# The seam between two layers of a graph network: part of the next matrix ahead of the last row tile, other work moved between the outputs

## The chip, the cores and the metric

The kernel runs on one core of one Trainium2 chip. The metric is the device time in microseconds (us) of one execution; the time of a kernel is the median of several runs.

## The reference, cut to what matters

625 nodes with 768 features pass four residual layers. Layers 0, 1 and 3 are graph attention layers, layer 2 is three relational convolutions. Every layer begins with a normalization of the whole input row, so a row tile of the next layer's input exists only when that row tile of this layer's output does.

```python
h = jnp.maximum(_layernorm(x, axis=-1), 0.0)
x = x + _L1_gnn_ref(h, edge_index, ...)            # attention, 4 heads of 512, then 1 head of 768
h = jnp.maximum(_layernorm(x, axis=-1), 0.0)
x = x + _L2_gnn_ref(h, node_type_3, edge_index, edge_type_3, ...)
# in _L2: h = concat([x, node_emb[node_type]], -1); then three times
xw = jnp.einsum('nd,rde->rne', h, w_rel)           # 3 relations
msg = xw[edge_type, src] * inv[dst, edge_type][:, None]
h = relu(segment_sum(msg, dst) + h @ w_root + bias)
```

## The kernel before

The 625 nodes are five row tiles of 125. Edges have been counted into dense matrices, so aggregation is a matrix product. Float32 products are split in a high and a low part: ACT copies the high part (lines L1131 for weights, L1247 for layer inputs), POOL subtracts the low part of weights (L1042), DVE the low part of everything that comes out of PSUM (L1451), and TensorE (PE) multiplies three times.

One list of steps (`STEPS`) is walked by all engines, each taking its own part of every step **in the order of the list**. No scheduler moves anything: an engine that waits for one step does nothing of a later one. `gat_steps` writes the list of an attention layer, and its last phase is the seam of this case. For the last head each row tile `t` goes through `mask_rows`, `score_rows` (DVE, L1795 and L1803), `softmax` (ACT exp, L1287) and `attention_T` (PE transposes, L786; ACT and DVE copy into `AT`). `tick` writes these for one `t`, `attention_T` coming three ticks behind. Then for each tile `d` come two steps:

- `output` d: PE multiplies (L832, 30 matmuls). ACT has a DMA bring the old x of tile d+1 into one of two buffers `xl`; POOL adds the bias (L1095); DVE makes the new rows `xo` (L1848) and their statistics; POOL makes the scale (`nb`, L1074); ACT makes the normalized rows `hn` (L1174) and stores x.
- `norm_T` d: PE transposes `hn` (L842, and in layer 1 also L847, which picks two nodes), ACT copies the high part and DVE the low part into `XB` (layer 0) or `XA` (layer 1). The low part of a tile raises "input lo" for it.

In the list `output` d+1 stands ahead of `norm_T` d. So on ACT the rows `hn` of tile 4 stand ahead of the high part of tile 3. The matrix of the next layer (L756) begins when all five tiles are there: 240 matmuls of 256 columns after layer 0, and after layer 1 the step `relation` 0 of the first convolution, 105 matmuls of 384 columns. Between layer 1 and `relation` 0 stands `embed`: DVE makes the operands of the node type embedding in a dozen small instructions (from L1860), PE multiplies them (L900), ACT and DVE put the result into `XA`, and then DVE counts the columns of relation 0 (`count_columns`, L1516 and L1502), ahead of the low part of the rows of `relation` 0 (`Hl`, L1451). PE needs the PSUM banks that this last step frees for the transposes `degrees` (L793) and the counted columns for `mean_T`, which come next.

Weights come through a ring `stage` (three tiles of 384) and a ring `pairs` (five tiles of 384); the step `split` says how far ACT and POOL may split them. In layer 1 all five are split at tick 5. At `output` 0 of layer 1 ACT also starts the DMA `cr_in` (2.3 MB of edge counts) in the same queue as the x tiles.

## Time and profile before

| | us |
|---|---|
| median of 3 runs | 1867.71 |
| range of the runs | 1866.33 to 1869.11 |
| the profiled execution: its own time | 1865.71 |
| its span | 1863.9 |
| PE busy | 1560.5 |
| DVE busy | 859.0 |
| ACT busy | 585.0 |
| POOL busy | 533.1 |

The span is what the profile's rows lie in. 1.8 us of the own time lie around it. Starts in the rows are us from the start of the span.

### The profile page before, as it was taken

What the parts mean: (1) busy time and instruction counts of PE and PEld (TensorE: products, weight loads), DVE (VectorE), ACT (ScalarE), POOL (GpSimd) and SP (SyncE); (2) the same over time, 40 slices, a digit from 0 to 9 for tenths busy, and PEclk for the clock granted to TensorE, in tenths of its full rate; (3) what the DMA queues carried; (4) which work ended last, traced back from release to release, by engine and by line L of the source; (5) the groups of instructions that cost most, each with busy time, mean ns of one, the idle gap of its engine ahead of it and who ended that gap; (6) DMA issues with size and microseconds to landing.
All of it is one profiled execution on the core that took longest, in us unless ns stands there. A gap on an engine that the chain in (4) does not pass through costs nothing.

```text
span 1863.9 us, 27128 instructions
## 1 busy us (share of the span) xinstructions
PE 1560.5 (84%) x10165; PEld 1505.3 (81%) x10165; DVE 859.0 (46%) x2156; ACT 585.0 (31%) x1170; POOL 533.1 (29%) x681
## 2 busy tenths in 40 slices
PE   4985889996778898975999999999999996566777
PEld 3655889996778898975999999999999986456777
DVE  5786676314266763144644223140423133677633
ACT  2224343322234433222332222322221222355421
POOL 3233332232233322313222333323231322222122
PEclk9997899997888999986999999999999997767797
DMA  2221111122211101222111122112123222100012
GB/s 87 72 75 37 44 46 29 45 76 62 75 51 46 46 29 46 75 80 87 48 30 49 52 60 61 55 52 58 57 61 86 74 88 72 31 1 1 5 47 86
DMA packets 87923, 101.63 MB, mean 55 GB/s; under 512 B 9477, under 2 KB 80418, under 8 KB 87796
## 3 DMA queue, kind: packets, MB, share of 16 engines
q1 hardware_dynamic: 71290, 68.86, 12.8%
q10 hardware_dynamic: 16506, 31.07, 5.0%
q8 instruction: 81, 1.33, 0.3%
q14 instruction: 46, 0.38, 0.1%
HBM read 88.12 MB, written 11.78 MB: 54 GB/s over the span
## 4 chain that ended last, share of the span: by engine, by line
PE 62%; DVE 11%; issue 9%; DMA 7%; ACT 6%; POOL 3%; ACTq 0%; DVEq 0%; POOLq 0%; SPq 0%
PE ps L756 35%; PE ps L819 7%; PE ps L931 6%; PE ps L913 4%; DMA xl<-x_scratch 3%; PE ps L786 3%; DVE junk L1748 2%; DVE prob L1795 2%; PE ps L889 2%; DMA stage<-in_W 2%; DMA xl<-in_x 1%; PE ps L952 1%; POOL pairs L1042 1%; ACT pairs L1131 1%; PE ps L975 1%
## 5 line engine op out<-in xcount | busy, mean ns | idle before, releaser
L1042 POOL TENSOR_TENSOR pairs<-stage,pairs 128x256 fp32r<-128x256 f32 (+3 forms) x472 | 367.0, 795 | 891.5 <-ACT pairs L1131 890.5
L756 PE MATMUL ps<-pairs,XB 128*125 128x256 f32 (+2 forms) x2880 | 424.2, 309 | 23.2 <-issue 8.1
L756 PEld LDWEIGHTS ps<-pairs,XB 128*125 128x125 f32 (+1 forms) x2880 | 413.9, 197 | 27.5 <-issue 10.2
L756 PE MATMUL ps<-pairs,XA 128*125 128x256 f32 (+3 forms) x2655 | 378.0, 304 | 7.1 <-DVE asp L1748 6.0
L756 PEld LDWEIGHTS ps<-pairs,XA 128*125 128x125 f32 (+2 forms) x2655 | 373.1, 190 | 9.2 <-DVE asp L1748 6.4
L1131 ACT ACTIVATE pairs<-stage 128x256 fp32r<-128x256 f32 (+3 forms) x472 | 189.7, 424 | 580.8 <-PE ps L756 416.5
L819 PE MATMUL ps<-AT,Hg 125*128 125x314 f32 (+1 forms) x1080 | 168.3, 317 | 13.9 <-ACT asb L1272 7.3
L819 PEld LDWEIGHTS ps<-AT,Hg 125*128 125x128 f32 (+1 forms) x1080 | 162.7, 191 | 15.8 <-ACT asb L1272 8.1
L1451 DVE TENSOR_TENSOR Hl<-ps,Hl 125x768 fp32r<-125x768 f32 (+3 forms) x57 | 43.6, 818 | 271.0 <-ACT Hl L1181 271.0
L786 PE MATMUL ps<-ident,prob 125*125 125x125 f32 x475 | 89.8, 348 | 85.9 <-ACT full L1189 33.2
L786 PEld LDWEIGHTS ps<-ident,prob 125*125 125x125 f32 x475 | 80.5, 253 | 92.0 <-issue 39.8
L1089 POOL TENSOR_SCALAR prob<-prob,rden 125x625 f32<-125x625 f32 x80 | 81.0, 1012 | 227.2 <-DVE rden L1811 227.2
L931 PE MATMUL ps<-MT,Hl 125*128 125x314 f32 (+1 forms) x780 | 115.4, 308 | 0.0
L931 PEld LDWEIGHTS ps<-MT,Hl 125*128 125x128 f32 (+1 forms) x780 | 113.8, 189 | 0.0
L832 PE MATMUL ps<-Hg,AT 125*125 125x384 f32 x450 | 90.7, 363 | 9.4 <-DVE AT L1451 9.4
L832 PEld LDWEIGHTS ps<-Hg,AT 125*125 125x125 f32 x450 | 86.6, 204 | 10.7 <-issue 8.3
L1451 DVE TENSOR_TENSOR Hg<-ps,Hg 125x1024 fp32r<-125x1024 f32 (+3 forms) x24 | 18.6, 819 | 157.9 <-ACT Hg L1181 157.9
L1795 DVE SCALAR_TENSOR_TENSOR prob<-asb,ad 125x626 f32<-125x626 f32 x95 | 85.0, 895 | 12.7 <-ACT asb L1272 12.7
L1803 DVE CUSTOM_DVE_ANT_0 prob<-prob,lnc 125x626 f32<-125x626 f32 x95 | 87.2, 918 | 1.6
L1451 DVE TENSOR_TENSOR AT<-ps,AT 125x625 fp32r<-125x625 f32 x75 | 58.4, 800 | 62.4 <-ACT AT L1215 62.4
L1287 ACT ACTIVATE prob<-prob,mx 125x626 f32<-125x626 f32 x95 | 77.1, 812 | 31.7 <-DVE mx L1803 21.3
L1897 DVE TENSOR_TENSOR scaled<-ps,degrees 128x628 f32<-128x628 f32 x39 | 31.6, 810 | 105.0 <-PE ps L931 104.9
(210 smaller groups left out, 1696.5 us busy)
## 6 DMA issues: line engine op xcount, KB each, us to landing
stage<-in_W SPq DMA_DIRECT2D x192, 128.0 KB, 2.3
stage<-in_rel SPq DMA_DIRECT2D x99, 192.0 KB, 2.4
stage<-in_root SPq DMA_DIRECT2D x91, 64.0 KB, 1.8
x_scratch<-xo ACTq DMA_DIRECT2D x15, 375.0 KB
xl<-x_scratch ACTq DMA_DIRECT2D x15, 375.0 KB
stage<-in_rel SPq DMA_DIRECT2D x42, 128.0 KB, 2.1
stage<-in_root SPq DMA_DIRECT2D x12, 192.0 KB, 2.4
stage<-in_W SPq DMA_DIRECT2D x12, 192.0 KB, 2.5
```

Of the source, the lines that this page charges most:

```text
L756: last = mm(o, X[:rows, xi, a, P * (s0 + t):P * (s0 + t) + m], pair(n, b), start=k == 0 and i == 0 and t * pitch % BANK == 0, stop=k == le ...
L786: last = nc.tensor.transpose(slot(q)[:m, 128 * j:128 * j + P], M[:, d, P * j:P * j + m], ident[:P, :P])
L819: last = mm(halves(q, m)[:, c, :], Hg[:, t, a, c0:c0 + m], att_of(l, h)[:P, t, b, HC * c:HC * c + HC], start=t == 0 and i == 0, stop=t == ...
L832: last = mm(halves(q, P, 384)[:, c, :], AT[:, t, a, P * d:P * d + P], Hg[:, t, b, 384 * c:384 * c + 384], start=t == 0 and i == 0, stop=t ...
L931: last = mm(halves(q, 128)[:, half, :], Hl[:rows, t, r, a, 128 * f:128 * f + 128], MT[:rows, r, t, HC * half:HC * half + HC], start=t == 0 ...
L1042: nc.gpsimd.tensor_tensor(pair(n, 1), staged(n), pair(n, 0).bitcast(F32), ALU.subtract).then_inc(*up("weights_lo", "weights lo", n))
L1089: nc.gpsimd.tensor_scalar(prob[:, d, :N], prob[:, d, :N], rden[:, d:d + 1], 1.0, ALU.mult, ALU.mult).then_inc(*up("prob_ready", "rows read ...
L1131: A(pair(n, 0), staged(n), ACT.Copy).then_inc(*up("weights_hi", "weights hi", n))
L1287: A(prob[:, d, :N + 1], prob[:, d, :N + 1], ACT.Exp, bias=mx[:, d:d + 1], scale=-1.0, accum_out=den[:, d:d + 1]).then_inc(*up("exp_ready", ...
L1451: return V.tensor_tensor(out_ap, whole, hi_ap.bitcast(F32), ALU.subtract)
L1795: V.scalar_tensor_tensor(out=prob[:, d, :N + 1], in0=asb[:, 0, :N + 1], scalar=ad8[:, heads_order[l, h] % 2, d:d + 1], in1=asb[:, 1, :N + ...
L1803: V.tensor_tensor_reduce(out=prob[:, d, :N + 1], in0=prob[:, d, :N + 1], in1=lnc[:, d, :N + 1], scale=-1.0, scalar=-FLOOR, op0=ALU.add, op ...
```

## The change

The list of steps is written differently at the ends of layers 0 and 1; nothing is computed differently.

- `early`: the first matrix of the next layer begins with its first four weight tiles (`EARLY_K`) on row tiles 0 to 3, after `norm_T` 3 and ahead of `norm_T` 4. `late` does these four weight tiles for row tile 4 after `norm_T` 4; the rest follows as before. `early` does not signal its weights as used, `late` does.
- The lag of `attention_T` is two ticks and not three, in layers 0 and 1.
- In layer 1 three tiles of relation weights are split after tick 1 (`split_to`), the other two at tick 5 as before.
- In layer 1 the operands of the embedding are made between `output` 3 and `output` 4 (`embed_operands`) with their own buffers. The product, its copy and `count_columns` stay in `embed`.

```diff
@@ gat_steps @@
-    for t in range(NT + 3):
-        yield from tick(l, h, t)
+    lag = 3 if l == 3 else 2
+    for t in range(NT + lag):
+        yield from tick(l, h, t, lag)
+        if l == 1 and t == 1:
+            yield ("split_to", ("relation", 1, 0, 0, 384), STAGED // WMAX)
         if l == 1 and t == 5:
             yield ("split", ("relation", 1, 0, 0, 384), 0)
         if t >= 4:
             yield ("output", l, t - 4)
             if t > 4 and l != 3:
                 yield ("norm_T", l + 1, t - 5)
-    yield ("output", l, NT - 1)
+    for d in range(NT + lag - 4, NT):
+        if l == 1 and d == NT - 1:
+            yield ("embed_operands",)
+        yield ("output", l, d)
+        if l != 3 and d < NT - 1:
+            yield ("norm_T", l + 1, d - 1)
     if l != 3:
+        first = FIRST_MATRIX[l + 1]
         yield ("norm_T", l + 1, NT - 2)
+        yield ("early", first)
         yield ("norm_T", l + 1, NT - 1)
+        yield ("late", first)
@@ PE @@
+                                if g == mine[0]:
+                                    ready = source_ready(s, k)
+                                    if kind == "early":
+                                        ready = (*ready[:2], NT - 2)
...
-                        else:
+                        elif kind != "early":
                             last.then_inc(*up("weights_used", "weights used", n))
@@ DVE @@
-                elif kind == "embed":
+                elif kind == "embed_operands":
                     dve.wait_ge(*at("node ids"))
...
                     V.tensor_copy(nth[:, N:N + CLONES], most[:R, :]).then_inc(*up("embed", "embed operands"))
+                elif kind == "embed":
+                    V.memset(degrees[:, :, N:NP], 0.0)
                     V.memset(XA[:, 0:6, :, N + CLONES:NP].bitcast(F32), 0.0).then_inc(*up("embed", "XA pad"))
                     dve.wait_ge(*at("embed hi"))
```

**What stands where, PE.** The end of layer 1 on PE before, from `output` 4 to the end of `relation` 0; a row is line, operation, written tile and read tiles, shape and count. `hn` is transposed in `norm_T` 3 and then 4, L900 is the embedding's product.

```order
L832 MATMUL ps<-Hg,AT 125x384 x30
L842 MATMUL ps<-ident,hn 128x125 x6
L847 MATMUL ps<-pickc,hn 128x2 x6
L842 MATMUL ps<-ident,hn 128x125 x6
L847 MATMUL ps<-pickc,hn 128x2 x6
L900 MATMUL ps<-nth,emh 128x314 x4
L756 MATMUL ps<-pairs,XA 125x384 x24
```

The same place now.

```order
L867 MATMUL ps<-Hg,AT 125x384 x30
L877 MATMUL ps<-ident,hn 128x125 x6
L882 MATMUL ps<-pickc,hn 128x2 x6
L791 MATMUL ps<-pairs,XA 125x384 x48
L877 MATMUL ps<-ident,hn 128x125 x6
L882 MATMUL ps<-pickc,hn 128x2 x6
L791 MATMUL ps<-pairs,XA 127x384 x12
L935 MATMUL ps<-nth,emh 128x314 x4
```

48 matmuls stand ahead of `norm_T` 4, and the embedding's product comes behind the 12 of row tile 4. After layer 0 it is the same with 48 and 12 matmuls of 256 columns, without L882 and L935.

**What stands where, DVE.** The end of layer 1 on DVE before, from `xo` of tile 4: statistics, low part of tile 3, low part of tile 4, and the first rows of the embedding's operands.

```order
L1848 SCALAR_TENSOR_TENSOR xo<-ps,rden,xl 125x768
L1436 BN_STATS bns<-xo 125x6 x2
L1439 BN_AGGR mv<-bns 125x2
L1571 TENSOR_TENSOR xc<-ps,xc 128x12
L1451 TENSOR_TENSOR XA<-ps,XA 128x6x125
L1571 TENSOR_TENSOR xc<-ps,xc 128x12
L1451 TENSOR_TENSOR XA<-ps,XA 128x6x125
L1583 CAST XA<-xc 128x6x2
L1451 TENSOR_TENSOR XA<-xc,XA 128x6x2
L1860 CAST scaled<-node_74 128x628
```

The last row of the operands now (the others stand ahead of it), and what follows.

```order
L1913 CAST nth<-most 3x2
L1883 SCALAR_TENSOR_TENSOR xo<-ps,rden,xl 125x768
L1471 BN_STATS bns<-xo 125x6 x2
L1474 BN_AGGR mv<-bns 125x2
L1606 TENSOR_TENSOR xc<-ps,xc 128x12
L1486 TENSOR_TENSOR XA<-ps,XA 128x6x125
L1606 TENSOR_TENSOR xc<-ps,xc 128x12
L1486 TENSOR_TENSOR XA<-ps,XA 128x6x125
L1618 CAST XA<-xc 128x6x2
L1486 TENSOR_TENSOR XA<-xc,XA 128x6x2
L1915 MEMSET degrees 128x3x3
L1916 MEMSET XA 128x12
```

The operands moved ahead of `xo` of tile 4. The embedding's copy and the counting of columns still come behind all of this.

**What stands where, ACT.** The last rows of layer 1 on ACT now: high part of tile 2, `hn` of tile 4, its store, and the high parts of tiles 3 and 4. Before it was the same order.

```order
L1282 ACTIVATE XA<-ps 128x6x125
L1209 ACTIVATE hn<-xo,nb,rstd 125x768
L1201 DMA x_scratch<-xo 125x768
L1282 ACTIVATE XA<-ps 128x6x125 x2
L1404 ACTIVATE XA<-ps 128x628
```

Nothing moved here: the high part of tile 3, for which `early` waits, stands behind `hn` of tile 4.

## Rows read from the trace of the kernel before

**Rows 1.** the page: first line, and the chain that ended last, by line

```profile
span 1863.9 us, 27128 instructions
...
PE ps L756 35%; PE ps L819 7%; PE ps L931 6%; PE ps L913 4%; DMA xl<-x_scratch 3%; PE ps L786 3%; DVE junk L1748 2%; DVE prob L1795 2%; PE ps L889 2%; DMA stage<-in_W 2%; DMA xl<-in_x 1%; PE ps L952 1%; POOL pairs L1042 1%; ACT pairs L1131 1%; PE ps L975 1%
```

**Rows 2.** PE in time, end of layer 0: start, length, what, [idle before]

```profile
447.93 8.10 PE L832 MATMUL ps<-Hg,AT 125*125 125x384 f32 x30 [2.51 <-DVE AT L1451]
...
492.55 1.49 PE L842 MATMUL ps<-ident,hn 125*128 125x125 f32 x6 [7.45 <-ACT hn L1174]
495.95 31.09 PE L756 MATMUL ps<-pairs,XB 128*125 128x256 f32 x240 [1.92 <-DVE XB L1451]
```

**Rows 3.** ACT in order of time, end of layer 0

```profile
491.38 1.03 ACT L1174 ACTIVATE hn<-xo,nb,rstd 125x768 f32<-125x768 f32 x1 [7.10 <-POOL nb L1074]
...
492.31 0.78 ACT L1247 ACTIVATE XB<-ps 128x750 fp32r<-128x750 f32 x1
```

**Rows 4.** DVE in order of time, end of layer 0

```profile
493.12 0.94 DVE L1451 TENSOR_TENSOR XB<-ps,XB 128x750 fp32r<-128x750 f32 x1 [3.17 <-ACT XB L1247]
```

**Rows 5.** chain that ended last, in order of time, layer 0

```profile
475.77 9.90 DMA xl<-in_x
```

**Rows 6.** busy time, PEclk and DMA in stretches of 10 us

```profile
500.00:510.00 10.00, 10.00 (x81) 10.00 (x81) 0.00 (x0) 2.54 (x7) 3.36 (x5) 0.93 0.19 54
910.00:920.00 10.00, 9.83 (x59) 9.60 (x60) 8.07 (x21) 5.54 (x14) 0.00 (x0) 0.83 0.07 22
```

**Rows 7.** PE in order of time, end of layer 1 and relation 0

```profile
855.20 1.39 PE L786 MATMUL ps<-ident,prob 125*125 125x125 f32 x5
856.25 7.12 PE L832 MATMUL ps<-Hg,AT 125*125 125x384 f32 x30
...
871.09 1.40 PE L847 MATMUL ps<-pickc,hn 125*128 125x2 f32 x12
...
886.33 1.38 PE L900 MATMUL ps<-nth,emh 3*128 3x314 f32 x4 [6.88 <-DVE XA L1880]
887.64 20.05 PE L756 MATMUL ps<-pairs,XA 128*125 128x384 f32 x105
...
910.05 2.12 PE L793 MATMUL ps<-ident,inv 125*128 125x125 f32 x10 [1.83 <-DVE Hl L1451]
...
915.81 18.73 PE L756 MATMUL ps<-pairs,XA 128*125 128x384 f32 x105
```

**Rows 8.** DVE in order of time, end of layer 1 and relation 0

```profile
869.04 0.93 DVE L1451 TENSOR_TENSOR XA<-ps,XA 128x750 fp32r<-128x750 f32 x1
870.70 1.02 DVE L1848 SCALAR_TENSOR_TENSOR xo<-ps,rden,xl 125x768 f32<-125x768 f32 x1 [0.73 <-issue]
...
876.27 0.93 DVE L1451 TENSOR_TENSOR XA<-ps,XA 128x750 fp32r<-128x750 f32 x1
...
881.54 0.48 DVE L1860 CAST scaled<-node 128x628 f32<-128x628 int32 x1
...
888.47 0.81 DVE L1451 TENSOR_TENSOR XA<-ps,XA 128x628 fp32r<-128x628 f32 x1 [2.27 <-ACT XA L1369]
...
902.10 0.23 DVE L1525 SCALAR_TENSOR_TENSOR mean<-mean,once,column 125x5 f32<-125x5 f32 x1
909.04 2.29 DVE L1451 TENSOR_TENSOR Hl<-ps,Hl 125x768 fp32r<-125x768 f32 x3 [6.71 <-ACT Hl L1181]
```

**Rows 9.** DVE in order of time, start of layer 1's last phase

```profile
819.05 2.00 DVE L1803 CUSTOM_DVE_ANT_0 prob<-prob,lnc 125x626 f32<-125x626 f32 x1
```

**Rows 10.** POOL in order of time, the same place

```profile
818.57 1.81 POOL L1095 TENSOR_TENSOR xl<-xl,b2b 125x768 f32<-125x768 f32 x1 [25.97 <-DMA xl<-x_scratch]
```

**Rows 11.** chain that ended last, in order of time, layer 1

```profile
818.07 26.54 DMA xl<-x_scratch
```

**Rows 12.** ACT in order of time, end of layer 1

```profile
874.44 1.03 ACT L1174 ACTIVATE hn<-xo,nb,rstd 125x768 f32<-125x768 f32 x1 [5.52 <-POOL nb L1074]
...
875.37 0.78 ACT L1247 ACTIVATE XA<-ps 128x750 fp32r<-128x750 f32 x1
```

More of the change, by code:

```diff
@@ L42 @@
 PASSES = ((0, 0), (0, 1), (1, 0))
+EARLY_K = 4
+FIRST_MATRIX = {1: ("project", 1, 0, 256), 2: ("relation", 1, 0, 0, 384)}
 EXACT = 4096.0
@@ L84, in tick @@
         yield ("softmax", l, h, t - 1)
-    if 3 <= t < NT + 3:
-        yield ("attention_T", l, h, t - 3)
+    if lag <= t < NT + lag:
+        yield ("attention_T", l, h, t - lag)
 def rows_of(s):
@@ L324, in weight_tiles, with begin @@
 def weight_tiles(I):
-    out, begun = {}, {}
+    out, begun = {}, dict.fromkeys(FIRST_MATRIX.values(), EARLY_K)
+    def begin(s, tiles):
+        if s in FIRST_MATRIX.values():
+            out["early", s] = tiles[:EARLY_K]
     for l, (heads, dh) in GAT_HEADS.items():
@@ L339, in weight_tiles @@
             if s[0] in ("project", "project2"):
+                begin(s, tiles)
                 k0, k1 = part or (begun.get(s, 0), len(tiles))
@@ L346, in weight_tiles @@
             f0 = RGCN_CHUNKS[i][c][0]
-            out[s] = [(I[f"rel_{i}"][r, 128 * k:128 * k + 128, f0:f0 + w], 128, w) for k in range(RGCN_IN[i])]
+            tiles = [(I[f"rel_{i}"][r, 128 * k:128 * k + 128, f0:f0 + w], 128, w) for k in range(RGCN_IN[i])]
+            begin(s, tiles)
+            out[s] = tiles[begun.get(s, 0):]
         if s[0] == "combine":
@@ L364, in build @@
         for s in STEPS:
-            whole = s[1] if s[0] == "part" else s
+            whole = s[1] if s[0] in ("part", "early") else s
             first_tile.setdefault(whole, len(W))
@@ L370, in build @@
                 begun[whole] = s[3]
+            if s[0] == "early":
+                begun[whole] = EARLY_K
         def ring(columns):
@@ L398, in split_limit @@
         def split_limit(s):
+            if s[0] == "split_to":
+                return first_tile[s[1]] + s[2]
             if s[0] == "split":
@@ L724, in _ @@
                 kind = s[0]
-                if kind in ("project", "project2", "relation", "part"):
-                    k_from, k_to = s[2:] if kind == "part" else (begun.get(s, 0), None)
-                    if kind == "part":
+                if kind in ("project", "project2", "relation", "part", "early", "late"):
+                    k_from, k_to = ((0, EARLY_K) if kind in ("early", "late") else
+                                    s[2:] if kind == "part" else (begun.get(s, 0), None))
+                    if kind in ("part", "early", "late"):
                         s = s[1]
@@ L732, in _ @@
                     gs = groups(w)
-                    qs = [fill_of["rows", s, g] for g in range(len(gs))] if k_from else []
+                    mine = range(len(gs) - 1) if kind == "early" else (
+                        range(len(gs) - 1, len(gs)) if kind == "late" else range(len(gs)))
+                    qs = ([fill_of["rows", s, g] for g in range(len(gs))] if k_from else
+                          [fill_of["rows", s, g] for g in range(len(gs) - 1)] if kind == "late" else [])
                     waited = None
@@ L736, in _ @@
                         block_k = range(k0, min(k0 + 2, k_to or len(src)))
-                        for g, (s0, ns, pitch) in enumerate(gs):
+                        for g in mine:
+                            s0, ns, pitch = gs[g]
                             if k0 == 0:
                                 qs.append(acquire("rows", s, g, banks=-(-ns * pitch // BANK)))
-                                if kind == "part":
+                                if kind in ("part", "early", "late"):
                                     held.update(range(place[qs[g]], place[qs[g]] - (-ns * pitch // BANK)))
@@ L746, in _ @@
                                     pe.wait_ge(*at("clones in"))
[L747 to L749 removed]
+                                if g == mine[0]:
+                                    ready = source_ready(s, k)
+                                    if kind == "early":
+                                        ready = (*ready[:2], NT - 2)
+                                    if ready != waited:
+                                        waited = ready
                                         pe.wait_ge(*at(*waited))
@@ L1493, in sum_relations, with pick_columns @@
                     *up("repeats", "repeats in", d))
-            def pick_columns(out_of, rows, n):
+            def pick_columns(out_of, rows, n, picked=picked):
                 for j in range(CLONES):
@@ L1555, in _ @@
                 if kind not in ("mask_rows", "score_rows", "softmax", "attention_T", "aggregate", "elu", "elu_high", "combine", "relation_sum", "part",
-                                "split") or (kind == "attention_T" and s[1] < 3):
+                                "split", "split_to", "early", "late") or (kind == "attention_T" and s[1] < 3):
                     finish_tile()
@@ L1857, in _ @@
                         stats(n, xo[:, i % 2, :])
-                elif kind == "embed":
+                elif kind == "embed_operands":
                     dve.wait_ge(*at("node ids"))
-                    V.tensor_copy(scaled[:, 0, :], node32[:, :]).then_inc(*up("embed", "nodes float"))
-                    V.memset(degrees[:, :, N:NP], 0.0)
+                    V.tensor_copy(nodesf[:, :], node32[:, :]).then_inc(*up("embed", "nodes float"))
                     dve.wait_ge(*at("nodes float"))
                     for j in range(CLONES):
-                        V.tensor_scalar(pick[:, j, :], scaled[:, 0, :], pick_id[:, j:j + 1], None,
+                        V.tensor_scalar(pick[:, j, :], nodesf[:, :], pick_id[:, j:j + 1], None,
                                         ALU.is_equal).then_inc(*up("embed", "pick rows", j))
```

13 lines of the change are left out of this document (6 added, 7 removed).

## The prediction

> **What bounds the kernel now.** I began with the page. The chain that ended last is mostly TensorE's own work: L756, the big projections, is 35% of the span [rows 1], so a change that saves no matmul can only win what PE loses in waits. The change touches two places, so I read PE in order of time at each, and then the engine that it waits for.
>
> After layer 0, PE waits 7.45 us for the normalized rows `hn` of tile 4 and 1.92 us more for that tile's low part, then does the 240 matmuls in 31.09 us [rows 2]. The work that could fill the long wait is not there: on ACT the high part of tile 3 (492.31) runs right behind `hn` of tile 4 (491.38) [rows 3], and the low part of tile 3 ends at 493.12 + 0.94 = 494.06 [rows 4], after PE's long wait is over. `hn` of tile 4 itself hangs on the DMA of its x, 9.90 us long [rows 5], one of a cycle through two buffers. Behind a wait PE's granted clock is at 1.2 instead of 2.4 GHz for some us: at 0.93 over the stretch 500 to 510, and 0.83 in 910 to 920 behind a wait of only 1.83 us [rows 6, 7].
>
> After layer 1 there are the waits of `norm_T` 4, then 6.88 us for the embedding's operands, and after `relation` 0 one of 1.83 us for DVE's `Hl` [rows 7]. DVE meanwhile goes through `xo` 4, the operands, the embedding's copy (888.47), counting until 902.10 + 0.23, and `Hl` [rows 8]. The counting ends 5.4 us ahead of the end of `relation` 0 (887.64 + 20.05). That is a cover which the change can use up.
>
> **The change, layer 0.**
> *Lag of two.* `output` 0 waited 2.51 us for the low part of `AT` 0 [rows 2]. Now that copy stands ahead of a later tile's scores, and the third `attention_T` (as long as the 1.39 us of one at low clock [rows 7]) goes into the wait. 2.51 - 1.39, less 0.3 for handing over, is 0.8 us. I take 0.7, since part of it is repaid if the clock rises at the same moment (0.4 to 0.9). It reaches the end, because the cycle of x loads starts with `hn` 0.
> *Early and late.* `early` can start at 494.1 and not during the 7.45 us; that is 1.9 us ahead of 495.95. But `norm_T` 4 now comes behind it: 0.8 us (1.49 at low clock [rows 2], half of that at full), and then PE again waits for ACT and DVE to copy tile 4, 1.9 us as before, since what `late` needs is that copy. So +0.8 on balance. And this second wait comes when the clock is up: behind 1.83 us the stretch shows 0.83, so 0.17 x 10 x 2 = 3.4 us at half clock, which costs 1.7 [rows 6]. I take +2.4 (0.8 without the second fall, 2.9 if the first rise comes 1 us later too).
> Layer 0: **+1.7** (-0.1 to +2.5).
>
> **The change, layer 1.**
> *Start of the phase.* Three weight tiles are now split on ACT between exp 0 and exp 1 and on POOL beside DVE's scores; `AT` 0's copy (0.8) also stands ahead of the fourth scores, and the third `attention_T` ahead of the DMA of the edge counts. No row shows how late these make that DMA. The nearest: a score row on DVE (819.05) took 2.00 us beside a POOL operation of 1.81, and ended 0.67 behind that one's end (820.38) [rows 9, 10]. I take 1.5 us later. The x of tile 1 is queued behind these counts: 26.54 us from issue to landing [rows 11], and all outputs from 1 on wait for it. Against it, three transfers of weights leave the time of that transfer, which I put at 0.5 us. **+1.0** (-0.5 to +2.5; below zero if the DMA is issued as early as now).
> The Trainium skill, SBUF — State Buffer, section "Who interferes with whom", says that DVE with two SBUF inputs and GpSimd hold their shared port in turn for a whole instruction. The 2.00 us above agree. By that rule alone three splits of about 1 us could hold DVE for 3 us, and the sum below would be 1.5 higher.
> *The transposes of tile 4* (855.20, 1.39) no longer lie between `norm_T` 1 and `output` 3 (856.25) [rows 7]: 1.05 us, of which I count 0.8, because that output began at low clock.
> *The operands of the embedding* take from 881.54 to 886.2, 4.7 us [rows 7, 8]. They now stand ahead of `xo` 4 and behind the low part of tile 2, which ended at 869.97; DVE then had only 0.73 us of idle time before `xo` 4 at 870.70 [rows 8]. Now: 869.97 - 0.8 + 4.7 = 873.9, so `xo` 4 is **3.2 later**. That is the stall which the 6.88 turn into.
> *The way to early.* From `xo` 4 to `hn` 4 are 3.74 us, the high part of tile 3 follows at 875.37 [rows 12], and its low part ends at 877.20, 6.5 behind `xo` 4 [rows 8]. Now 880.4. `early` has 48 of the 105 matmuls that took 18.73 us [rows 7]: 8.6, and 2.0 for starting at low clock (the first 105 took 1.3 longer, with the embedding's product ahead of them): until 891.0. `norm_T` 4 is 2.05 at full clock: 1.40 for the picks [rows 7] and 0.65 for the transposes, a little under half of 1.49 [rows 2]: 893.0. ACT, DVE and the copies for the two picked nodes: 2.2 (1.9 after layer 0, and two small ones): `late` at 895.2. Its 12 matmuls are 2.1, the embedding's product 0.7, and 0.8 for half of a clock fall: 898.8.
> *Relation 0.* PE has 45 matmuls left, 8.0 us, and about 1 us of waiting for weight tile 5, whose place comes free only with `late`: 907.8, where it was 907.7. So for PE nothing is won or lost here. But DVE decides. It copies the embedding 1.6 us behind its product (from 886.33 + 1.38 to 888.47 + 0.81 [rows 7, 8]): 900.4. Then it counts, 889.28 to 902.33, 13.05 us: 913.4. `Hl` comes behind that, its first third takes 0.8: 914.2. PE's `degrees` need its banks. Before, the second five of them began at 910.05 and 5.76 us later the next relation (915.81) [rows 7]; now five more come ahead (0.8): 915.1, and the next relation at 920.9. **+5.1** (+3.5 to +6.7: 1.6 either way, for where the clock rises and falls in `early` and `late`). All from `xo` 4 on is in this number, the 0.8 and the 3.2 too.
> Layer 1: **+6.1** (3.0 to 9.2).
> The other edits cost nothing: POOL's two iotas run ahead of a bias addition that DVE now asks for 3 us later, and the two tiny loads have 10 us to land. DVE's count for the next relation has that relation's whole 18.73 us to hide under, and no copy of the embedding ahead of it.
>
> **The sum.** 1.7 + 6.1 = 7.8, from 2.9 to 11.7. The profiled execution's own time was 1865.71: 1873.5. The median of the runs is 2.0 above it, so the runs should give **1875.5**, and with the bounds 1870.6 to 1879.4.
>
> **The rivals.**
> *The waits are really filled (faster).* If the low part of tile 3 were there before `hn` of tile 4, 48 matmuls at 0.123 (81 in the 10 us of 500 to 510 [rows 6]) would fit into the 7.45: -5.9 at layer 0. At layer 1 they would run from 872, `late` would start at about 885, DVE's count would end at 903.5, and the gain would be 4.9. With -0.7 and +1.0: -10.5, 1857.2. The 7.45 and 6.88 of idle speak for it; the order on ACT and its rows speak against it [rows 3, 12]. It decides from where tile 3's copy comes 5 us ahead of `hn` 4. Chance 0.13, with everything that makes it faster by less.
> *The counting stays under `relation` 0 (no change).* If neither clock falls a second time, the counts' DMA is no later and DVE counts faster with fewer splits beside it, the low ends hold: +2.9, and 2 us less for a count that ends with the relation: 1868.6. That PE's own path is even speaks for it, 13.05 us of counting against it. Chance 0.17.
> *The x of tile 1 comes much later (slower still).* If exp 1, the transposes and the scores all wait for the splits, the counts start 4 us later: 1878. It is the high end of the forecast.
> The forecast itself, slower by more than 0.2%: 0.70. About 0.2% (3.7 us) is what a measurement of this kernel tells from none.
>
> **Range.** The forecast's own is 1870.6 to 1879.4. With one us of scatter above, and down into the case of no change, 1867 to 1880.5 leaves out the faster case and little else.
>
> **What would show it.** `early` starts right behind the low part of tile 3, itself behind `hn` 4, in both layers, and PE's wait for `hn` 4 in layer 0 is still about 7 us. Behind `norm_T` 4 stands a new wait of about 2 us with PEclk falling. `xo` 4 of layer 1 begins at the end of the operands, some 4 us behind the end of `output` 3's chain. PE waits some 5 us for `Hl` behind `relation` 0, where it waited 1.83. The prediction is wrong if `early` runs inside the old waits, if DVE has finished counting when `relation` 0 ends, or if x 1 lands no later than at 844.6 and everything behind it moves up.

## The result, and the profile after

The changed kernel takes 1881.04 us (median of 4 runs, 1878.20 to 1883.19), the kernel before 1867.07 beside it: 1.0073 times as long, 95% interval 1.0060 to 1.0085, so +14.0 us. The forecast was slower, +7.8 us, with a range up to 1880.5: the direction is right, the size is not, and the median lies 0.5 above the range.

The page of the changed kernel (first line, chain by line), beside [rows 1]:

```profile
span 1876.4 us, 27128 instructions
...
PE ps L791 35%; PE ps L854 7%; PE ps L966 6%; PE ps L948 4%; DMA xl<-x_scratch 3%; PE ps L821 3%; DVE junk L1783 2%; DVE prob L1830 2%; PE ps L924 2%; DMA stage<-in_W 2%; PE ps L987 1%; DMA xl<-in_x 1%; PE ps L1010 1%; ACT pairs L1166 1%; POOL pairs L1077 1%
```

As many instructions, a span 12.5 us longer, and nearly the same shares. (L756 of before is L791 now, and the later lines have moved by about 35.) The page does not tell where the time went; PE in order of time does. End of layer 0, beside [rows 2]:

```profile
445.94 6.98 PE L867 MATMUL ps<-Hg,AT 125*125 125x384 f32 x30
...
490.38 7.34 PE L791 MATMUL ps<-pairs,XB 128*125 128x256 f32 x48 [8.89 <-issue]
497.55 0.81 PE L877 MATMUL ps<-ident,hn 125*128 125x125 f32 x6
500.27 24.49 PE L791 MATMUL ps<-pairs,XB 128*125 128x256 f32 x192 [1.91 <-issue]
525.41 0.78 PE L810 MATMUL ps<-ident,asad 125*125 125x125 f32 x5 [0.64 <-DVE asad L1809]
```

`output` 0 waits for nothing now (2.51 before). But the 48 early matmuls begin behind a wait of 8.89 us, not inside the old one. (`<-issue` names no releaser; DVE's low part of tile 3 runs from 489.34 to 490.28, and they begin 0.1 us behind it.) ACT in order of time shows why, as it did before [rows 3]: the high part of tile 3 (488.53) is behind `hn` of tile 4 (487.59).

```profile
487.59 1.03 ACT L1209 ACTIVATE hn<-xo,nb,rstd 125x768 f32<-125x768 f32 x1 [6.39 <-POOL nb L1109]
...
488.53 0.78 ACT L1282 ACTIVATE XB<-ps 128x750 fp32r<-128x750 f32 x1
```

I measure a phase from the `spread` of its start (the five transposes of `asad`), since executions reach it at different times: in the traces of this case the `spread` of layer 0 begins between 436.08 and 440.50. Layer 0's last phase, spread to spread, was 90.82 us and is 89.33: 1.5 **shorter**.

PE in order of time, from the start of layer 1's last phase to the second relation, beside [rows 7]:

```profile
807.06 1.38 PE L810 MATMUL ps<-ident,asad 125*125 125x125 f32 x5 [5.93 <-DVE asad L1806]
...
853.26 1.49 PE L877 MATMUL ps<-ident,hn 125*128 125x125 f32 x6 [11.64 <-ACT hn L1209]
...
883.11 10.06 PE L791 MATMUL ps<-pairs,XA 128*125 128x384 f32 x48 [9.15 <-issue]
893.01 0.81 PE L877 MATMUL ps<-ident,hn 125*128 125x125 f32 x6
...
897.33 4.18 PE L791 MATMUL ps<-pairs,XA 128*127 128x384 f32 x12 [2.27 <-DVE XA L1486]
901.44 1.41 PE L935 MATMUL ps<-nth,emh 3*128 3x314 f32 x4
902.78 10.13 PE L791 MATMUL ps<-pairs,XA 128*125 128x384 f32 x45
922.12 3.36 PE L828 MATMUL ps<-ident,inv 125*128 125x125 f32 x15 [9.22 <-issue]
...
928.78 16.44 PE L791 MATMUL ps<-pairs,XA 128*125 128x384 f32 x92
```

(The view ends inside the last row; the second relation has 105 matmuls.) From spread to the second relation are 121.72 us (807.06 to 928.78), where the trace before has 107.60: **+14.1**. DVE in order of time has the reason of both long waits, beside [rows 8]:

```profile
870.51 0.93 DVE L1486 TENSOR_TENSOR XA<-ps,XA 128x750 fp32r<-128x750 f32 x1
871.36 0.97 DVE L1895 CAST nodesf<-node 128x628 f32<-128x628 int32 x1
...
876.51 1.02 DVE L1883 SCALAR_TENSOR_TENSOR xo<-ps,rden,xl 125x768 f32<-125x768 f32 x1
...
882.08 0.93 DVE L1486 TENSOR_TENSOR XA<-ps,XA 128x750 fp32r<-128x750 f32 x1
896.01 0.93 DVE L1486 TENSOR_TENSOR XA<-ps,XA 128x750 fp32r<-128x750 f32 x1
...
904.39 1.02 DVE L1551 TENSOR_SCALAR mean<-cr_in 125x625 f32<-125x625 uint16 x1
905.34 1.61 DVE L1537 CUSTOM_DVE_ANT_0 picked<-cr_in,pick 125x625 bf16<-125x625 uint16 x1
...
909.63 0.80 DVE L1537 CUSTOM_DVE_ANT_0 picked<-cr_in,pick 125x625 bf16<-125x625 uint16 x1
...
919.60 0.23 DVE L1560 SCALAR_TENSOR_TENSOR mean<-mean,once,column 125x5 f32<-125x5 f32 x1
919.74 2.28 DVE L1486 TENSOR_TENSOR Hl<-ps,Hl 125x768 fp32r<-125x768 f32 x3
```

The operands (871.36 to 876.49) stand between the low part of tile 2 and `xo` 4, and the count (904.39 to 919.83) ends 7 us behind the end of `relation` 0's matmuls (912.9), where it ended 5.4 us ahead of them. A `picked` takes 1.61 us in some places and 0.80 in others. POOL in order of time shows what lies beside the long ones:

```profile
904.07 3.76 POOL L1077 TENSOR_TENSOR pairs<-stage,pairs 128x384 fp32r<-128x384 f32 x3 [23.85 <-ACT pairs L1166]
```

At the start of the phase, ACT with its DMA queue (ACTq), in order of time:

```profile
820.35 0.28 ACTq L1390 DMA_DIRECT2D cr_in<-relation_counts  x1
820.73 7.32 ACTq L1186 DMA_DIRECT2D xl<-x_scratch  x1
```

The DMA of the edge counts is issued 13.29 us behind the spread (9.48 before), the load of x 1 behind it, and that load lands 25.6 us later: `hn` 1 comes 45.0 us behind the spread, 42.1 before.

### The profile page after: what moved, and what is told of

Read it like the earlier page. It is cut to its first block, busy times and chain, and to the rows that moved or that the text cites. A ratio compares the mean times of both kernels' runs of the same rounds, so it can differ in the third digit from the quotient of the medians.

```text
span 1876.4 us, 27128 instructions
## 1 busy us (share of the span) xinstructions
PE 1563.8 (83%) x10165; PEld 1506.0 (80%) x10165; DVE 862.9 (46%) x2156; ACT 584.7 (31%) x1170; POOL 537.7 (29%) x681
## 4 chain that ended last, share of the span: by engine, by line
PE 61%; DVE 12%; issue 9%; DMA 7%; ACT 6%; POOL 3%; ACTq 0%; DVEq 0%; POOLq 0%; SPq 0%
PE ps L791 35%; PE ps L854 7%; PE ps L966 6%; PE ps L948 4%; DMA xl<-x_scratch 3%; PE ps L821 3%; DVE junk L1783 2%; DVE prob L1830 2%; PE ps L924 2%; DMA stage<-in_W 2%; PE ps L987 1%; DMA xl<-in_x 1%; PE ps L1010 1%; ACT pairs L1166 1%; POOL pairs L1077 1%
## 5 line engine op out<-in xcount | busy, mean ns | idle before, releaser
L1077 POOL TENSOR_TENSOR pairs<-stage,pairs 128x256 fp32r<-128x256 f32 (+3 forms) x472 | 370.9, 803 | 916.0 <-ACT pairs L1166 915.0
L791 PE MATMUL ps<-pairs,XB 128*125 128x256 f32 (+2 forms) x2880 | 424.8, 309 | 31.3 <-issue 18.6
L791 PEld LDWEIGHTS ps<-pairs,XB 128*125 128x125 f32 (+1 forms) x2880 | 414.2, 197 | 35.7 <-issue 21.7
L791 PE MATMUL ps<-pairs,XA 128*125 128x256 f32 (+3 forms) x2655 | 382.0, 306 | 18.6 <-issue 9.1
L791 PEld LDWEIGHTS ps<-pairs,XA 128*125 128x125 f32 (+2 forms) x2655 | 375.7, 191 | 21.3 <-issue 10.1
```

Of the source, the lines that this page charges most:

```text
L791: last = mm(o, X[:rows, xi, a, P * (s0 + t):P * (s0 + t) + m], pair(n, b), start=k == 0 and i == 0 and t * pitch % BANK == 0, stop=k == le ...
L1077: nc.gpsimd.tensor_tensor(pair(n, 1), staged(n), pair(n, 0).bitcast(F32), ALU.subtract).then_inc(*up("weights_lo", "weights lo", n))
```

## The experiments

Sixteen kernels, in four groups; a group shares its runs of the kernel before, whose median was 1867.06, 1867.52, 1867.28 and 1867.98. A difference to the kernel before is to the median of its own group; where a kernel is set against the changed one, that one's 1881.04 is meant. "In company" means together with the other edits.

**One part of the change alone.** Each kernel is the one before with one edit of the diff shown above: the lag; `early` and `late`; `embed_operands` moved; `split_to`.

> The kernel before with the lag of two alone. Theory (each engine works its steps in order, and the parts add): output 0 of layer 0 begins about 2 us earlier (445.9 instead of 447.9), the clock rises earlier in it, and hn 4 comes 3.8 us earlier as in the changed kernel; without early and late all of this reaches the 240 matmuls: -3.8 us at the end of layer 0, of which about 1 us may be lost later. In layer 1 the counts' DMA is issued up to 1 us later, and the transposes of tile 4 leave PE's path: about 0. In all -2 to -4 us. Rival (the shift comes from elsewhere and the lag is worth the 0.7 us of the prediction): -0.7 us, hn 4 at 490.5 or later.

> The kernel before with early and late alone (lag of three, operands of the embedding behind late). Theory: early begins right behind the low part of tile 3 (494.1 in layer 0, 877.3 in layer 1), norm_T 4 and a wait of about 2 us follow, with the clock falling: +1.5 to +2.4 in layer 0. In layer 1 late starts at about 892, the operands take 4.7 us on DVE, the count of columns runs until about 914 and PE waits for Hl: the second relation starts 6 to 8 us later. In all +8 to +10 us. Rival (early fills waits and only the other parts cost): 0 or a gain.

> The kernel before with the operands of the embedding between output 3 and output 4 alone. Theory: xo 4 of layer 1 begins 4 to 5 us later, the wait of 6.88 us for the operands is gone, relation 0 starts 1 to 2 us earlier: -1 to -2 us, and DVE's count is still done before relation 0 ends. Rival (moving the operands is what costs, by delaying xo 4): +3 to +4 us.

> The kernel before with the first three relation weights split after tick 1 alone. Theory (POOL's splits stand in the way of DVE's scores, so the DMA of the counts and the x of tile 1 behind it are late): scores take 1.5 to 1.6 us instead of 0.9 and 0.8 us, the counts' DMA is issued about 2.5 us later, hn 1 comes 2 to 2.5 us later, +2 to +2.5 us. Rival (the transfer of the counts is shorter by the weights that no longer run beside it): 0 or -1 us.

Measured: lag 1863.31 (-3.75; ratio 0.9973 to 0.9992), early and late 1875.19 (+8.1; 1.0026 to 1.0054), operands 1863.82 (-3.2; 0.9970 to 0.9990), split 1870.14 (+3.1; 1.0006 to 1.0025). The expectations had the right sign in all four; the operands won more than the 1 to 2 us expected, the split cost more than the 2 to 2.5. They add up to +4.2, not to +14.0. By phases, from the traces (in us, against the kernel before):

| | lag | early | operands | split | sum | all together |
|---|---|---|---|---|---|---|
| layer 0, spread to spread (90.82) | -3.0 | +1.6 | -0.3 | +0.2 | -1.5 | -1.5 |
| layer 1, spread to second relation (107.60) | +0.4 | +7.9 | -2.8 | +3.15 | +8.65 | +14.1 |

In layer 0 the parts add up. In layer 1 5.5 us come from company. A hint is in PE's wait for the operands, in order of time, with early and late alone:

```profile
902.83 1.38 PE L932 MATMUL ps<-nth,emh 3*128 3x314 f32 x4 [0.42 <-DVE XA L1913]
```

Before it was 6.88 us. With the early matmuls in front, DVE makes the operands while PE is busy, and there is nothing left that moving them could win.

**The change less one part.** In order: the count moved on DVE, the counts' DMA moved on ACT's queue, the split left out, the operands put back.

```diff
-  (DVE, at "embed")      count_columns(0)
+  (DVE, at "early" of the relation)   count_columns(0)
```
```diff
-                    if (l, d) == (1, 0):        # ahead of load_x(i + 1)
+                    if (l, d) == (1, 3):        # behind load_x(i + 1)
                         act.dma_start(cr_in[...], cr_scr[...])
```
```diff
-        if l == 1 and t == 1:
-            yield ("split_to", ("relation", 1, 0, 0, 384), STAGED // WMAX)
```
```diff
-        if l == 1 and d == NT - 1:
-            yield ("embed_operands",)
 def rgcn_steps():
+    yield ("embed_operands",)
     yield ("embed",)
```

> The changed kernel with one edit: DVE counts the columns of the first relation's block right behind its low part of tile 3 in layer 1 (where it is idle for 12.9 us in the changed kernel, 882.99 to 895.9), and no longer behind the copy of the embedding. Theory (the 9.22 us that TensorE waits for Hl behind relation 0 are the count, which lost its place under relation 0, and no weight splits of GpSimd run beside it in the new place): the count of about 13 us delays the low part of tile 4 by at most 1 us, TensorE's wait for Hl falls from 9.2 to between 1 and 3 us, and the time falls by 5.5 to 8, to about 1874 where the changed kernel has 1881. Rival (TensorE's wait for Hl is really for the weights that ACT and GpSimd split): the wait stays above 7 us and the time within 2 us of 1881.

> The changed kernel with one edit: the DMA of the edge counts (cr_in) is issued on ACT's queue in output 3 of layer 1, behind the load of x 4, and no longer in output 0 ahead of the load of x 1. Theory (the x of tile 1 sits behind this transfer, and hn 1 comes as late as it lands): hn 1 comes within 25 us of the spread of layer 1 where it was 45.0 us, TensorE's wait of 11.6 us ahead of norm_T 1 is gone, and the phase is at least 9 us shorter: about 1870 or less where the changed kernel has 1881. Rival (the x of tile 1 is late by itself, because the write of x and its reload take that long with the weights in flight): hn 1 stays beyond 40 us and the time within 3 us of 1881. Second rival: the transfer moved stands before the x of the embedding or the weights of relation 0, and the wait returns there; then the phase gains less than 5 us.

> The changed kernel without the early split of three relation weights (split_to). If the split costs the same with the other edits as alone (+3.1 us, by the DMA of the edge counts being issued 3.6 us later), the time is 1878, and that DMA is issued about 10 us behind the spread where it was 13.3. If the split is what the early matmuls of relation 0 need (weights ready in time), the time is above 1881 and TensorE waits for weights inside the early 48 matmuls.

> The changed kernel with the embedding's operands made again behind everything of layer 1, as in the kernel before, all other edits kept. Alone this edit of the change gained 3.2 us, because TensorE waited for the operands. Theory (with the early matmuls in front, that wait is already down to 0.4 us, so that the operands between outputs only delay xo 4 by about 4 us): the time is 3 to 6 us below the changed kernel, 1875 to 1878, and hn 4 comes about 4 us earlier relative to hn 1. Rival (the edits add up as they stand alone): the time rises by 3, to 1884.

Measured: 1873.59, 1872.00, 1877.57 and 1876.51, that is -7.5, -9.0, -3.5 and -4.5 against the changed kernel's 1881.04 (by layer 1's phase -6.4, -9.3, -2.5 and -3.8). The ratios to the kernel before are 1.0017 to 1.0040, 1.0014 to 1.0034, 1.0038 to 1.0072 and 1.0032 to 1.0065. The last two overlap with the changed kernel's own (1.0060 to 1.0085), so for the split and the operands it is the phases that tell.

*The count.* In its new place it takes 10.0 us, from 883.83 to 893.81, its end 3 us ahead of tile 4's copy (897.08). DVE in order of time, all of them short, with no split beside them:

```profile
883.83 0.43 DVE L1551 TENSOR_SCALAR mean<-cr_in 125x625 f32<-125x625 uint16 x1
884.18 0.81 DVE L1537 CUSTOM_DVE_ANT_0 picked<-cr_in,pick 125x625 bf16<-125x625 uint16 x1
...
893.58 0.23 DVE L1560 SCALAR_TENSOR_TENSOR mean<-mean,once,column 125x5 f32<-125x5 f32 x1
```

PE's wait for `Hl` falls from 9.22 to 3.74 us, a little more than the 1 to 3 expected. The rival, the weights, is out.

*The operands.* Taken out of the changed kernel they win 4.5 us, where put in alone they also won 3.2. So moving them is worth -3.2 without the early matmuls and +4.5 with them, a swing of 7.7 (6.6 by the phases), which covers the 5.5 that company costs in layer 1 (the other edits together come 1.1 cheaper than alone). PE in order of time, that version:

```profile
879.84 10.49 PE L790 MATMUL ps<-pairs,XA 128*125 128x384 f32 x48 [4.82 <-issue]
```

The wait ahead of `early` is 4.82 where it is 9.15 with the operands between the outputs.

*The split* costs about as much in company as alone (2.5 and 3.15 by the phases), while the counts' DMA stands ahead of x 1.

*The counts' DMA.* `hn` 1 comes 32.9 instead of 45.0 us behind the spread, counted to tile 1's own `hn` (841.93 - 809.04), 12.1 earlier; the "within 25 us" of the expectation was too much. POOL adds the bias to x 1 at 836.30, without waiting for a DMA, right behind the two weight splits of tick 5 (834.36 to 836.34), so `hn` 1 hangs on these now. PE's wait of 11.6 us is down to 2.2. But the phase won only 9.3. ACT's queue, in order of time, shows the rest:

```profile
849.85 0.34 ACTq L1392 DMA_DIRECT2D cr_in<-relation_counts  x1
...
857.54 6.83 ACTq L1201 DMA_DIRECT2D x_scratch<-xo  x1
864.41 0.80 ACT L1282 ACTIVATE XA<-ps 128x750 fp32r<-128x750 f32 x1 [5.84 <-issue]
```

The next issue behind the 2.29 MB of counts takes 6.83 us, and ACT stands still for it: its copy of tile 2 comes at 864.41, and DVE's operands and `xo` 4 behind that.

**Where early could pay, and where the counts belong.** `norm_T` of tile 3 ahead of output 4; the counts in output 4; then two versions put together.

```diff
     for d in range(NT + lag - 4, NT):
+        if l != 3 and d == NT - 1:
+            yield ("norm_T", l + 1, NT - 2)
         yield ("output", l, d)
...
-        yield ("norm_T", l + 1, NT - 2)
         yield ("early", first)
```
```diff
-                    if (l, d) == (1, 3):
+                    if (l, d) == (1, 4):
                         act.dma_start(cr_in[...], cr_scr[...])
```

> The changed kernel with one edit: in both layers norm_T of tile 3 (transposes, high part on ACT, low part on DVE) stands ahead of output 4 and no longer behind it. Theory (the early matmuls do not fill TensorE's wait because ACT makes tile 3's copy behind hn 4): now that copy is made before hn 4, the early matmuls start right behind output 4's, and TensorE's wait ahead of them (8.9 us in layer 0, 9.2 in layer 1) falls below 2 us. Price: in layer 1 output 4 waits 2 to 3 us for hn 3. Sum: layer 0 -5.9 (48 matmuls inside the wait), layer 1 -5 to -6: about 1870 where the changed kernel has 1881. Rival (the early matmuls cannot pay, because what follows hn 4 hangs on the DMA of x 4 and the clock falls a third time): the time stays above 1877.

> The changed kernel with the DMA of the edge counts issued one output later still, in output 4 behind hn 4. In output 3 it kept ACT's next issue (the write of hn 3's x) waiting for 6.83 us, ACT's copy of tile 2 stood behind that, and the embedding's operands and xo 4 behind the copy. Theory (that blocked issue is what the first move lost): no issue on ACT between hn 3 and hn 4 takes over 1 us, xo 4 comes 5 to 6 us earlier relative to the spread, and the time is 4 to 6 us below the run with the transfer in output 3 (1872.0), about 1867. Rival (the transfer then comes late for the count): DVE waits for it behind the embedding's copy, and the time is at or above 1872.

> The kernel before with three edits: lag of two in layers 0 and 1 (alone -3.7), the embedding's operands between outputs 3 and 4 of layer 1 (alone -3.2), and the DMA of the edge counts in output 4; no early matmuls, no early split of weights. If x 1 of layer 1 is late through that transfer alone, hn 1 comes 20 us earlier, PE's wait for it (14 us) goes, and the phase is 9 to 13 us shorter: 1848 to 1852. If ACT's queue of x loads is the bound by itself, it is 1860.

> The changed kernel with what the runs so far point to: norm_T of tile 3 ahead of output 4, the DMA of the edge counts in output 4, the count ahead of norm_T 4's low part, and no early split of weights. Theory (early matmuls pay once tile 3's copy is made before hn 4, and DVE's count has a place of its own): layer 0 -5.9 and layer 1 -5 beside the version without early matmuls, that is about 1840. Rival (the early matmuls only move waits): not below the version without them, 1850.

Measured: order 1870.29 (-10.8 to the changed kernel; ratio to before 1.0011 to 1.0030), counts in output 4 1866.84 (-14.2; 0.9992 to 1.0012), no early and no split 1857.20 (ratio to before 0.9922 to 0.9958), all with early 1866.25 (0.9985 to 1.0005).

*Order.* PE in order of time, layer 0 and then layer 1:

```profile
483.15 1.48 PE L878 MATMUL ps<-ident,hn 125*128 125x125 f32 x6 [6.38 <-ACT hn L1210]
484.29 6.28 PE L868 MATMUL ps<-Hg,AT 125*125 125x384 f32 x30
490.41 5.86 PE L792 MATMUL ps<-pairs,XB 128*125 128x256 f32 x48
...
865.71 1.49 PE L878 MATMUL ps<-ident,hn 125*128 125x125 f32 x6 [3.13 <-ACT hn L1210]
...
877.33 8.62 PE L792 MATMUL ps<-pairs,XA 128*125 128x384 f32 x48
```

The early matmuls follow output 4 without a wait. The waits of 8.9 and 9.2 us are gone, and in their place stand 6.38 and 3.13 for `hn` 3 ahead of output 4: the phases are 3.9 and 3.1 us shorter, not 5.9 and 5 to 6. So the early matmuls had won nothing because tile 3's copy came behind `hn` 4; with that mended, part of the wait moves to `hn` 3. (The profiled spans differ by 7.5 us, the medians by 10.8.)

*Counts in output 4.* As expected: 1866.84, against 1872.00 one output earlier (the phase of layer 1 takes 108.82 us, against 112.38).

*No early, no split.* 1857.20, where 1848 to 1852 was expected. The wait for `hn` 1 is 7.80 us, not gone (why, stands below). The counts, issued at 861.24, land only 24.5 us later, and DVE's count begins at 885.79, beside POOL's splits, and ends behind the relation: a wait of 2.75 us for `Hl`.

*All with early* missed by 26 us. Here the count stands ahead of tile 4's low part, and the counts come late. DVE and PE, in order of time:

```profile
881.38 0.49 DVE L1550 TENSOR_SCALAR mean<-cr_in 125x625 f32<-125x625 uint16 x1 [10.44 <-DMA cr_in<-relation_counts]
```
```profile
892.73 4.09 PE L790 MATMUL ps<-pairs,XA 128*127 128x384 f32 x12 [13.91 <-DVE XA L1485]
```

Two edits, each good alone, collide: a late transfer needs a late count, and the early count an early transfer. The mechanism of the expectation held in layer 0 (84.8 us from spread to spread), not in layer 1.

**What was still open.** The lag of three in the changed kernel (`return` to `tick(l, h, t, 3)` in layers 0 and 1); the kernel before with the counts in output 4; and two versions with `early` in layer 0 alone, the second with the counts in five pieces:

```diff
-FIRST_MATRIX = {1: ("project", 1, 0, 256), 2: ("relation", 1, 0, 0, 384)}
+FIRST_MATRIX = {1: ("project", 1, 0, 256)}
```
```diff
+                    if l == 1:                  # behind load_x(i + 1)
+                        act.dma_start(cr_in[:, d:d + 1, :]..., cr_scr[P * R * d:P * R * d + P * R]...)
```

> The changed kernel with the lag of three again in layers 0 and 1, all other edits kept. Alone the lag of two gained 3.75 us. If it gains the same in company, the time is 1884.8. If it is the part that loses 2 us by the company of the early split (exp 1 to 3 of layer 1 wait for DVE's scores beside GpSimd's splits, so that the third attention_T is no earlier), the time is 1882 to 1883. Below 1881 the lag of two would be a loss in company.

> The kernel before with one edit: the DMA of the edge counts in output 4 of layer 1. In the changed kernel the same edit gave 14 us (1881.0 to 1866.8), in the version without early matmuls the three edits together gave 10. Theory (this transfer on ACT's queue ahead of x 1 costs the kernel before too, some 4 to 10 us): 1858 to 1863, and hn 1 within 40 us of the spread. Rival (it only costs in company of the early split): 1867.

> The version with lag of two, moved operands and late counts (1857.2), with the early matmuls in layer 0 alone, where norm_T of tile 3 stands ahead of output 4. In the run with that order the phase of layer 0 was 85.4 us from spread to spread where it is 88.0 in this version, so 2.6 us less: 1854.6. Rival (early matmuls never pay): at or above 1857.

> The same version as the one before in this list, with the DMA of the edge counts in five pieces of one row tile, one in each output behind the load of the next x. Theory (the whole transfer takes 20 to 25 us to land, and ends up either ahead of an x or too late for the count; a piece of 458 KB fits between two x transfers): DVE counts without a wait and TensorE's wait of 2.75 us for Hl is gone, 1851 to 1853. Rival (pieces delay each write and load of x on ACT's queue by their own 4 to 5 us): above 1857.

Measured: lag of three 1882.11, counts late in the kernel before 1863.36 (ratio 0.9965 to 0.9985), early in layer 0 alone 1853.39 (0.9906 to 0.9939), the same with pieces 1852.46 (0.9898 to 0.9931).

*The lag.* +1.1 us where it is taken back, but both ratios carry some 2 to 3 us of interval, so the times don't tell 1.1 from 3.75. The phases tell more: layer 0 takes 92.81 with the lag of three against 89.33, layer 1 121.76 against 121.72. The lag of two wins 3.5 in layer 0 in company as alone (3.0), and nothing in layer 1, where x 1 decides. It doesn't explain the difference between 9.8 us of company by the medians and 5.5 by the phases; that part is as large as the scatter of the medians, and stays open.

*Counts late in the kernel before:* -4.6, 0.4 us outside of what was expected (1858 to 1863). So the same edit is worth 4.6 us in the kernel before and 14.2 in the changed one.

*Early in layer 0 alone* is 3.8 us better than without by the medians, whose intervals overlap. The phase of layer 0 tells more: it takes 85.41 us, and 88.00 in the version without early matmuls, which is the 2.6 expected. So early matmuls can pay. (Layer 1, which this edit doesn't touch, took 98.10 and 101.21; that part of the difference is not explained.) *Pieces:* 1852.46, which can't be told from 1853.39. PE's wait for `Hl` is 1.83 us in both, and in the version with pieces `hn` 4 comes later, 8.62 us of wait instead of 6.96. The time lies where it was expected (1851 to 1853), but neither theory was borne out: DVE no longer waits for the counts (5.9 us in the other version), which brought no gain, and the pieces cost no 4 us each.

*What holds `hn` 1 once the counts are late.* In all five kernels with the counts out of the way of x 1 and no early split PE still waits 7.3 to 8.0 us for `hn` 1; with the early split it waits 2.24 (changed kernel, counts in output 4). POOL in order of time, first the version with early in layer 0 alone, then the changed kernel with the counts in output 4:

```profile
828.81 2.94 POOL L1080 TENSOR_TENSOR pairs<-stage,pairs 128x384 fp32r<-128x384 f32 x3 [2.93 <-ACT pairs L1169]
833.93 1.97 POOL L1080 TENSOR_TENSOR pairs<-stage,pairs 128x384 fp32r<-128x384 f32 x2 [2.18 <-ACT pairs L1169]
835.86 1.80 POOL L1133 TENSOR_TENSOR xl<-xl,b2b 125x768 f32<-125x768 f32 x1
```
```profile
832.90 1.97 POOL L1077 TENSOR_TENSOR pairs<-stage,pairs 128x384 fp32r<-128x384 f32 x2 [2.93 <-ACT pairs L1166]
834.83 1.85 POOL L1130 TENSOR_TENSOR xl<-xl,b2b 125x768 f32<-125x768 f32 x1
```

POOL adds the bias to x 1 behind the splits of tick 5. Without the early split these are five, and the last two wait for their weights; with it they are two and wait for none. `hn` 1 comes 35.7 and 32.9 us behind the spread. So the early split, which cost about 3 us while x 1 hung on the counts, shortens this wait once x 1 does not. It is also a part of why late counts win 4.6 us in the kernel before (`hn` 1 38.4 us behind the spread) and 14.2 in the changed one. Late counts with the early split and without early matmuls in layer 1 were not run, so what the split is worth there is not shown.

## Why the prediction was right in direction and too small

**What held.** `early` started behind tile 3's low part, itself behind `hn` 4, in both layers, and the rival that forecast a gain fell by that. The second wait came (1.91 and 2.27 us; 1.9 and 2.2 said). `xo` 4 began at the end of the operands (876.51; operands until 876.49). From `xo` 4 to `early` 6.6 us (6.5 said), `early` 9.9 (10.6), `norm_T` 4 2.04 (2.05). The wait for `Hl` became the one that ends relation 0, by the count, as said (9.22 us, where some 5 were said).

**What failed** are sizes, not the order of events: the lag of two won about four times what it was given, and in layer 1 the start of the phase, the clock in `late`, the count and `Hl` all cost more. By the prediction's own steps:

- *"Lag of two": -0.7, measured -3.0* (alone; -3.5 in company). `output` 0 begins 9.86 us behind the spread instead of 11.07, 1.2 earlier. I then took off for the clock what is to be added: without a wait ahead of it the output runs in 6.98 us where it took 8.10, 1.1 less, and a wait of 1.55 us for `AT` ahead of output 4 (1.54 in the version with the lag of three) is gone too. `hn` 4 comes 3.0 earlier. Layer 0 got shorter by 1.5 where I had it 1.7 longer.
- *"Early and late", layer 0: +2.4, measured +1.6*: a right mechanism, a little dear.
- *"Start of the phase": +1.0, measured +2.9* at `hn` 1. The counts' DMA was issued 3.8 us later, not 1.5. I had priced one score row held by one POOL operation [rows 9, 10]. In the trace after, DVE in order of time and then POOL:

```profile
812.33 0.81 DVE L1838 CUSTOM_DVE_ANT_0 prob<-prob,lnc 125x626 f32<-125x626 f32 x1
...
813.07 1.60 DVE L1830 SCALAR_TENSOR_TENSOR prob<-asb,ad 125x626 f32<-125x626 f32 x1
...
814.70 1.49 DVE L1838 CUSTOM_DVE_ANT_0 prob<-prob,lnc 125x626 f32<-125x626 f32 x1
```
```profile
812.95 4.10 POOL L1077 TENSOR_TENSOR pairs<-stage,pairs 128x384 fp32r<-128x384 f32 x3 [21.49 <-ACT pairs L1166]
```

  Two more follow with 1.59 and 1.80 us (the last beside the bias addition of x). Without the split the first three take 0.87, 0.81 and 0.87. Four rows were held, not one. The Trainium skill, SBUF — State Buffer, section "Who interferes with whom", which calls the port shared by DVE and GpSimd an exclusive lock, had the sum 1.5 higher here and was the better guide: it would have given +2.5. With the split left out the changed kernel is 3.5 us faster.
- *"The operands": `xo` 4 3.2 later, with 0.8 for the transposes taken off already.* Measured 4.05 relative to `hn` 1 (operands 5.1 us instead of 4.7, since the first copy, 0.97, lies beside POOL, and of the 0.8 only 0.3 came: the low part of tile 2 ends 19.35 us behind `hn` 1, 19.64 before). And I counted PE's part as even, which it was only because the early matmuls had already taken away the 6.88.
- *"Relation 0": count 13.05, measured 15.4.* The same count is 10.0 us alone, 13.05 with four splits beside it (as before), 15.4 with seven: the splits moved into it together with the work.
- *"Its first third takes 0.8": 2.3.* PE's fifteen `degrees` began behind all three thirds of `Hl` (922.02), where before five ran ahead of it and ten behind its first third. That is so in every version with early matmuls in layer 1 and in none without them (3.74 us of wait even where the count is long done, against 1.83), so it is a price of `early` too; why the first five change places stays open.
- *`late` with the product: 3.6 said, 5.5 measured:* 12 matmuls took 4.18 us, where the last 39 in the version with late counts took 7.13 (0.18 each, 2.2 for 12): the whole of `late` and the product (897.3 to 902.8) had a granted clock of 0.50, 1.2 of 2.4 GHz, behind the second wait, and I had taken half of a fall. Windows of 10 us (the last three numbers are the granted clock, the DMA share and GB/s):

```profile
883.00:893.00 10.00, 9.89 (x48) 9.88 (x49) 0.01 (x1) 0.00 (x0) 0.00 (x0) 0.85 0.06 23
893.00:903.00 10.00, 7.73 (x36) 6.90 (x35) 1.32 (x6) 0.92 (x2) 0.00 (x0) 0.67 0.00 0
903.00:913.00 10.00, 9.84 (x45) 9.00 (x45) 9.39 (x14) 3.39 (x7) 7.65 (x6) 0.82 0.27 79
```

Added up for layer 1: start +1.9, `xo` 4 +0.9, the ways to `early` and to `late` +0.1 each, early -0.7, late and product +1.9, the embedding's copy 0 (its end came 1.6 behind its product, as said), count +2.35, `Hl` +1.45, together +8.0 over the +6.1 said, 14.1 as measured. Layer 0 gave 3.2 back. So the forecast of +7.8 becomes +12.6, and the profiled execution was 12.5 longer (1878.20 against 1865.71); that the medians lie 14.0 apart, 1.5 more, is within their interval (11.2 to 15.9).

**The largest thing that I did not ask** is how much the place of the counts' DMA was worth. The rows said it (26.54 us from issue to landing [rows 11], against 9.90 for an x without it [rows 5]), and I used them only for a shift. The Trainium skill, DMA: Bandwidth & Descriptors, section "Queues, rings and completion order", says that each DMA engine takes the descriptors of one ring in the order of the ring. The trace is in line with it: x 1 landed 25.6 us behind its issue with the counts ahead of it, and `hn` 1 came 12.1 us earlier with them behind.

## What to carry to other kernels

Work that is to fill a wait has to be ready before the wait begins: look on the engines that make its operands for what stands ahead of them in program order, here tile 3's copy behind `hn` 4, and move that first. Effects on one wait don't add: two edits that remove the same wait win once, and the second then costs its full price elsewhere. An edit that costs alone, as the early split, can shorten a wait once another one is gone. Before moving small things around a stall, ask of each large transfer ahead of the data that the stall waits for whether it must be there.

The version to keep (the one in pieces can't be told from it) is the kernel before with the lag of two, moved operands, counts in output 4, and early matmuls in layer 0 alone behind an earlier `norm_T` 3: 1853.39 us, 0.78% below before (0.61 to 0.94%).

## What the runs showed of the hardware

- The next DMA issue on ACT's queue behind 2.29 MB of counts took 7.32 us in the changed kernel, 6.83 with the counts in output 3 and 5.04 with the counts late in the kernel before; most other issues take 0.26 to 0.48. ACT's computing stood still for it where work was ready: 5.84 us in the second of these. In the changed kernel nothing was ready, and the next two issues took 2.57 and 4.64 us.
- The 2.29 MB landed 20.5 and 24.5 us after their issue beside other traffic, in two versions with the counts in output 4.
- DVE operations of 0.80 to 0.87 us on SBUF took 1.49 to 1.62 us beside GpSimd's splits, and 1.80 beside its bias addition. Seven splits so cost DVE's count 5.4 us (15.4 against 10.0).
- TensorE ran 48 matmuls of 256 columns in 5.86 us without a wait ahead of them, at a granted clock of 1.00, and in 7.34 behind one of 8.89 us, with 0.50 at first (490.4 to 492) and 1.00 from 494 on. 48 of 384 columns took 8.62 and, behind a wait of 9.15 us, 10.06.
